# One refinement step moved from the inverse to the right sides, in a DeltaNet and expert layer kernel

## The chip, the cores and the metric

One core of a Trainium2 chip runs the whole layer. The metric is the device time of one execution in microseconds.

## What is computed

The input is 2 sequences of 2048 tokens of 256 channels, cut into 32 chunks of 128 tokens. The layer is a gated delta-rule attention (16 value heads, 8 key heads, head size 128), followed by a mixture of 16 experts with 8 chosen and a shared one. The part that matters here is the recurrence:

```python
def step(state, inp):
    q_t, k_t, v_t, g_t, b_t = inp
    state = state * jnp.exp(g_t)[..., None, None]
    kv_mem = jnp.einsum('bhk,bhkv->bhv', k_t, state)
    delta = (v_t - kv_mem) * b_t[..., None]
    state = state + k_t[..., None] * delta[:, :, None, :]
    out = jnp.einsum('bhk,bhkv->bhv', q_t, state)
    return (state, out)
```

Within a chunk of 128 tokens the deltas of one head solve a triangular system (I + L) Z = R, where L holds the decayed products of the keys and R the right sides (values less what the carried state already gives). Everything is float32, and results have to agree with the float32 reference.

## The kernel before

The 16 value heads are worked on in 4 groups of 4. An *item* is one group of one chunk. In each item the program runs stages of several items at once, so that the engines overlap: `a` (projection, convolution taps, gates of the item three ahead), `f` (front: norms, key products, decays, the triangle L, two ahead), `i` (the inverse, one ahead), `s` (state: solve, output, new state, the item itself), `p` (output projection, one behind), and per chunk `c` (the next chunk's norm and betas) and `e` (experts of the chunk before). Each engine has its own function `item`, which writes its order out by hand; engines meet through semaphores, and every queue is strictly in order. The loop body holds 6 chunks and runs 5 times; the rest is unrolled before and behind it.

The inverse of I + L is built by doubling. GpSimd computes the inverses of the 16x16 diagonal blocks (`base_inverse`), which go through DRAM (`triangle_out`, `blocks_in`, `inverses_out`, `inverses_in`, issued by the sync engine), because the blocks have to change partitions. Three levels follow on TensorE. In each, `invert_q` multiplies, VectorE masks (`mask_q`), and `invert_xt` and `invert_x` add to the transposed inverse XiT and the inverse Xi, which ScalarE copies out of PSUM (`inverse_t`, `inverse`). `turned` (L566) multiplies it by the identity to get the inverse itself, `residual` (L573, L575) forms I - (I + L)X in plain float32 and one fp32r product, and `correct` (L582) adds X times this residual. VectorE copies the result to Tt (L1164), in float32.

The state stage takes two heads at a time (p = 0 and 1). `ks_qs` multiplies keys and queries with the state into banks bS and bD, `right_side` forms R (VectorE), `solve` multiplies by Tt in float32 (L604), `solved` copies Z (ScalarE), `az` and `new_state` form the output and the state's increment, `update_o` and `update_s` finish them on VectorE. `query_state` scales the queries' part on ScalarE. PSUM's eight banks are shared, so most steps also wait until the bank's last content has been read; expert steps, transposes and projections take turns on bB in the order B_ORDER.

## Time and profile before

| | |
|---|---|
| median of 3 runs | 3428.59 us (3428.09 to 3431.92) |
| the profiled execution's own time | 3419.12 us |
| its span, first to last instruction | 3417.3 us |
| mean granted TensorE clock | 0.984 |
| TensorE, VectorE, ScalarE, GpSimd busy | 94%, 80%, 71%, 63% |

An engine's busy time counts the time in which at least one of its instructions runs. TensorE's are pipelined: the next one starts long before the record of the last one ends, so its cost is the distance between starts. Lines such as L604 are lines of the kernel; an operation is named by what it writes and reads (bS<-R,Tt).

### The profile page before, as it was taken

To read this page: it belongs to the slowest core of one execution; us is meant where nothing else is said; L and a number is where in the kernel's file an instruction comes from. 1 tells how busy PE (TensorE), PEld (TensorE's weight loads), DVE (VectorE), ACT (ScalarE), POOL (GpSimd) and SP (SyncE) were. 2 spreads that over 40 slices of the span, in tenths; PEclk is the share of its full clock that TensorE was granted. 3 is DMA by queue.
4 is the path that set the end of the run, shared out by engine and by line. 5 is a ranking of instruction groups with operands and counts; after the bars stand their busy time and mean duration, and the time that the engine had idled before them with its cause. 6 is when DMAs were issued, how large, how long until landed. Compare 5 with 4: busy or idle time off the path is not lost.

```text
span 3417.3 us, 85191 instructions
## 1 busy us (share of the span) xinstructions
PE 3227.1 (94%) x23968; PEld 2867.9 (84%) x24096; DVE 2733.4 (80%) x8720; ACT 2417.5 (71%) x5922; POOL 2149.9 (63%) x5380
## 2 busy tenths in 40 slices
PE   4999999999999999999999999999999999999985
PEld 3888888888888888888888888888888888888874
DVE  4788888888888888788888878888888888888873
ACT  3777777776777777777777767777777777777762
POOL 2766666666666667566666666666666666666650
PEclk8999999999999999999999999999999999999996
DMA  4111111111111111111111111111111111111110
GB/s 179 37 44 37 44 39 34 44 41 39 40 44 34 44 41 37 37 47 35 38 47 37 37 45 38 38 46 39 37 46 35 39 44 41 36 44 38 38 42 4
DMA packets 424217, 145.70 MB, mean 43 GB/s; under 512 B 211168, under 2 KB 421664, under 8 KB 423200
## 3 DMA queue, kind: packets, MB, share of 16 engines
q1 hardware_dynamic: 423712, 139.83, 15.7%
q8 instruction: 211, 3.46, 0.4%
q14 instruction: 294, 2.41, 0.2%
HBM read 93.11 MB, written 46.66 MB: 41 GB/s over the span
## 4 chain that ended last, share of the span: by engine, by line
PE 66%; ACT 13%; issue 7%; DVE 6%; POOL 4%; DMA 3%; SPq 0%; POOLq 0%; ACTq 0%; DVEq 0%
PE bF L466 8%; PE bB L637 6%; PE bQ L547 5%; ACT L811 4%; PE bXT L555 4%; PE bB L693 3%; PE bS L604 3%; PE bB L687 3%; PE bF L477 3%; PE bF L479 3%; PE bD L619 3%; PE bS L612 3%; PE bS L596 2%; PE bX L560 2%; PE bD L597 2%
## 5 line engine op out<-in xcount | busy, mean ns | idle before, releaser
L1105 DVE SCALAR_TENSOR_TENSOR Y<-bF,Cv,Y 128x127 f32<-128x127 f32 (+2 forms) x3072 | 851.6, 339 | 8.2 <-ACT Y L828 3.1
L466 PE MATMUL bF<-XnT,Wqkv 128*128 128x128 f32 x4096 | 534.5, 278 | 0.5 <-ACT XnT L947 0.5
L466 PEld LDWEIGHTS bF<-XnT,Wqkv 128*128 128x128 f32 x4096 | 508.2, 194 | 9.7 <-issue 2.1
L828 ACT ACTIVATE Y<-bF,Cv 128x128 f32<-128x128 f32 x1024 | 385.8, 457 | 103.7 <-PE bF L466 100.3
L898 ACT ACTIVATE XiT<-bXT 128x512 fp32r<-128x512 f32 x384 | 229.0, 596 | 304.5 <-PE bXT L555 300.3
L1533 POOL TENSOR_TENSOR Tp<-Tp 32x64 f32<-32x64 f32 (+2 forms) x768 | 361.4, 471 | 60.2
L1148 DVE TENSOR_TENSOR Qi<-bQ,Cf 128x512 fp32r<-128x512 f32 x384 | 264.0, 688 | 97.7 <-PE bQ L547 96.3
L811 ACT ACT_TABLE_LOAD x257 | 329.7, 1283 | 5.3 <-PEq L1617 0.7
L555 PE MATMUL bXT<-Qi,Xi 128*128 128x128 f32 x1536 | 302.4, 319 | 2.4 <-DVE Qi L1148 2.4
L555 PEld LDWEIGHTS bXT<-Qi,Xi 128*128 128x128 f32 x1536 | 222.4, 192 | 96.4 <-DVE Qi L1148 47.3
L1526 POOL TENSOR_TENSOR Tp<-Yb,Tm 32x64 f32<-32x64 f32 (+1 forms) x384 | 275.4, 717 | 30.1
L1526 POOL TENSOR_TENSOR Tp<-Cb,Yb 32x64 f32<-32x64 f32 (+1 forms) x384 | 274.7, 715 | 30.5 <-POOL Yb L1535 0.8
L1541 POOL TENSOR_TENSOR Yb<-Cb,Cf 32x8 fp32r<-32x8 f32 x128 | 25.9, 202 | 414.4 <-DMA Cb<-DL 414.4
L547 PE MATMUL bQ<-XiT,LnR 128*128 128x128 f32 x1536 | 240.8, 279 | 19.5 <-ACT XiT L898 19.5
L547 PEld LDWEIGHTS bQ<-XiT,LnR 128*128 128x128 f32 x1536 | 211.9, 191 | 47.8 <-ACT XiT L898 28.8
L1427 POOL TENSOR_TENSOR Ln<-Ex,KKQ 128x512 f32<-128x512 f32 x128 | 164.1, 1282 | 129.6 <-issue 111.7
L637 PE MATMUL bB<-Wout,CoT 128*128 128x256 f32 x1024 | 244.2, 382 | 0.9 <-ACT CoT L934 0.8
L905 ACT ACTIVATE Xi<-bX 128x512 fp32r<-128x512 f32 x384 | 226.7, 590 | 2.8 <-PE bX L566 2.3
L1460 POOL TENSOR_TENSOR HG<-LnbG,Lnk 128x4 f32<-128x4 f32 x128 | 25.9, 203 | 299.1 <-ACT Lnk L861 299.1
L637 PEld LDWEIGHTS bB<-Wout,CoT 128*128 128x128 f32 x1024 | 185.9, 192 | 21.6 <-ACT CoT L934 1.1
L974 ACT ACTIVATE Rl<-bB 128x512 f32<-128x512 f32 x128 | 76.5, 597 | 158.4 <-PE bF L688 158.4
L604 PE MATMUL bS<-R,Tt 128*128 128x128 f32 x1024 | 166.8, 286 | 8.3 <-DVE Tt L1164 8.1
(198 smaller groups left out, 9338.8 us busy)
## 6 DMA issues: line engine op xcount, KB each, us to landing
DL<-Ln SPq DMA_DIRECT2D x128, 256.0 KB, 2.2
XiT<-DX SPq DMA_DIRECT2D x128, 256.0 KB, 2.7
Xi<-DX SPq DMA_DIRECT2D x128, 256.0 KB, 3.2
DX<-Yb SPq DMA_DIRECT2D x256, 32.0 KB, 1.9
Xf<-x SPq DMA_DIRECT2D x32, 128.0 KB, 2.8
Wqkv<-wqkv SPq DMA_DIRECT2D x4, 1024.0 KB, 18.0
Cb<-DL SPq DMA_DIRECT2D x128, 32.0 KB, 1.9
Xr<-x SPq DMA_DIRECT2D x32, 128.0 KB, 3.0
```

Of the source, the lines that this page charges most:

```text
L466: last = mm(bank[:, i, :], Wqkv[:, k, c:c + P], XnT[:, k, :], start=(k == 0), stop=(k == KT - 1))
L547: last = mm(heads(bQ)[:, h, :], LnR[:, h, :], XiT[:, h, :], start=True, stop=True)
L555: last = mm(heads(bXT)[:, h, :], Xi[:, h, :], Qi[:, h, :], start=False, stop=True, skip_group_check=True)
L604: last = mm(heads(bS)[:, i, :], Tt[:, 2 * p + i, :], R[:, i, :], start=True, stop=True)
L637: last = mm(bB[:, 0:HID], CoT[:, h, :], Wout[:, g * GH + h, :], start=(h == 0), stop=(h == GH - 1))
L811: nc.scalar.add_instruction(mybir.InstLoadActFuncSet(name=nc.get_next_instruction_name(), act_func_set_id=TABLES[name], engine=mybir.Engin ...
L828: last = op(Y[:, tile, :], bank[:, i, :], ACT.Identity, scale=c[:, TAPS - 1:TAPS], bias=c[:, TAPS:TAPS + 1])
L898: op(XiT[:, :, :], heads(bXT), ACT.Copy).then_inc(sem["xt_done"], 1)
L1105: last = stt(y, bank[:, i, 0:P - shift], Cv[:, g * TILES + tile, n:n + 1], y, ALU.mult, ALU.add)
L1148: tt(Qi[:, :, :], heads(bQ), level, ALU.mult).then_inc(sem["q_done"], 1)
L1526: then(tt(view(Tp[:, :], p * m ** 3, [[m * m, m], [m, m], [1, m]]), pair(left, p), pair(right, p), ALU.mult))
L1533: then(tt(lo, lo, hi, ALU.add))
```

## The change

The inverse is no longer refined. The third level adds to the inverse Xi instead of to its transpose, and ScalarE rounds it to Tt in fp32r (`inverted`). The refinement is made on the right sides: R is rounded to Rr (`rounded_r`), a first solve in fp32r gives Z (`first_z`), VectorE subtracts it from R (`left`), `check` multiplies -L by Z in plain float32, VectorE adds it (`residual`, rounded to Rr), and a second fp32r solve adds to the same bank (`correct`). The solve, the output and the state are done for four heads at once. The orders of TensorE, ScalarE and VectorE are written anew, and the experts' steps are spread differently over the items. Some buffers share memory (Hn with Xn, LaT with Rg), with the waits that this needs.

```diff
@@ sync: inverses_in
-                sp.wait_ge(sem["c_full"], at("c_full", ahead(f, -1)))
+                sp.wait_ge(sem["x_full"], at("x_full", ahead(f, -1)))
@@ tensor
             def invert_x(v, n):
+                if n == LEVELS - 1:
+                    pe.wait_ge(sem["q_done"], at("q_done", v))
+                    pe.wait_ge(sem["xi_done"], at("xi_done", v))
                 for h in range(GH):
                     last = mm(heads(bX)[:, h, :], Qi[:, h, :], Xi[:, h, :], start=False, stop=True, skip_group_check=True)
                 last.then_inc(sem["x_full"], 1)
-            def turned(v):
...
-            def residual(v):
...
-            def correct(v):
...
-            def solve(w, p):
...
+            def solve(w):
+                pe.wait_ge(sem["tt_done"], at("tt_done", w))
+                pe.wait_ge(sem["rr_done"], at("rr_done", w))
                 for h in range(GH):
+                    last = mm(heads(bS)[:, h, :], Tt[:, h, :], Rr[:, h, :], start=(h == 0), stop=True, skip_group_check=True)
+                last.then_inc(sem["zs_full"], 1)
+
+            def check(w):
+                pe.wait_ge(sem["z1_done"], at("z1_done", w))
+                pe.wait_ge(sem["qg_done"], at("qg_done", w))
+                pe.wait_ge(sem["neg_done"], at("neg_done", w))
                 for h in range(GH):
+                    last = mm(heads(bD)[:, h, :], Ln[:, w[1] % 2, h, :], Z[:, h, :], start=True, stop=True)
+                last.then_inc(sem["lz_full"], 1)
+
+            def correct(w):
+                pe.wait_ge(sem["rf_done"], at("rf_done", w))
                 for h in range(GH):
+                    last = mm(heads(bS)[:, h, :], Tt[:, h, :], Rr[:, h, :], start=False, stop=True, skip_group_check=True)
+                last.then_inc(sem["zf_full"], 1)
@@ scalar
+            def inverted(v):
+                act.wait_ge(sem["x_full"], at("x_full", v))
+                act.wait_ge(sem["zf_full"], at("zf_full", ahead(v, -1)))
+                op(Tt[:, :, :], heads(bX), ACT.Copy).then_inc(sem["tt_done"], 1)
+            def rounded_r(w):
+                act.wait_ge(sem["r_done"], at("r_done", w))
+                op(Rr[:, :, :], R[:, :, :], ACT.Copy).then_inc(sem["rr_done"], 1)
+
+            def first_z(w):
+                act.wait_ge(sem["zs_full"], at("zs_full", w))
+                op(Z[:, :, :], heads(bS), ACT.Copy).then_inc(sem["z1_done"], 1)
@@ vector
-            def refined(v):
...
+            def left(w):
+                dve.wait_ge(sem["z1_done"], at("z1_done", w))
+                tt(R[:, :, :], R[:, :, :], Z[:, :, :], ALU.subtract).then_inc(sem["left_done"], 1)
+
+            def residual(w):
+                dve.wait_ge(sem["lz_full"], at("lz_full", w))
+                dve.wait_ge(sem["left_done"], at("left_done", w))
+                tt(Rr[:, :, :], R[:, :, :], heads(bD), ALU.add).then_inc(sem["rf_done"], 1)
```

The new orders, with the stages' letters and the group in which a step of the chunk or the experts stands:

| engine | order in an item |
|---|---|
| TensorE | ks_qs; D2 (3); proj 0,0 and 0,1; ss; kkq; ktr; proj 1,0; **solve**; core_t; parts_t; vtr; exponents; **check**; hT (1); proj 1,1; invert_begin; q0; **correct**; gc (1); xt0; G1 (2), G3 (3); x0; ffn1 (1); q1; out_proj; xt1; D3 (3); x1; az; G0 (1); xnT (0); q2; D1 (2); new_state; laT (3); G2 (2); z_proj; D0 (1); ffo (3); x2; ba (0) |
| ScalarE | query_state; key_norm; **rounded_r**; last_tap 0; keys; ba (1); **first_z**; parts_t; core_t; scales; values; decays; hT (1); last_tap 1; XiT 0; ffn1 (1), G3 (3), G1 (2); Xi 0; norm (0); **solved**; XiT 1; norm1 (0); Xi 1; rounded_l; G0 (1), laT (3); square_o; G2 (2); xnT (0); activated; norm2 (0); ffo (3); out_norm; **inverted** |
| VectorE | ended; D0 (2); x1, ba, hn (1); right_side; squares; D2 (3); gated; products; taps; sp (1); **left; residual**; taps; mask 0; gc (1); taps; norm (0); shared (1); mask 1; scores (1); taps; U3 (3); accumulate; U1 (2); xn (0); D3, la (3); D1 (2); update_o; route (1), norm1 (0); update_s; U0 (1); mask 2; gate_bias; out_norm; ffo, result (3); U2 (2) |
| GpSimd | as before, but the scaled keys come behind the negated triangle |

Before, x1 and ba of VectorE stood at the end of group 0's item, D2 in group 2's, and `z_proj` had the third transposed product, xnT, `turned` and `residual` around and behind it.

## Rows read from the trace of the kernel before

**Rows 1.** The page's first part: busy us (share of the span) xinstructions of each engine.
```profile
PE 3227.1 (94%) x23968; PEld 2867.9 (84%) x24096; DVE 2733.4 (80%) x8720; ACT 2417.5 (71%) x5922; POOL 2149.9 (63%) x5380
```

**Rows 2.** Windows, one chunk and its four items: length, then each engine's busy us, PEclk.
```profile
1703.32:1805.47 102.15, 99.57 (x750) 88.74 (x753) 85.87 (x274) 75.42 (x186) 68.90 (x172) 1.00 0.16 40
1703.32:1727.86 24.54, 24.49 (x186) 21.91 (x186) 21.18 (x61) 17.89 (x43) 17.07 (x44) 1.00 0.15 37
1727.86:1751.61 23.75, 22.34 (x158) 19.44 (x158) 20.59 (x72) 17.42 (x47) 15.15 (x40) 1.00 0.19 50
1751.61:1779.19 27.58, 26.77 (x207) 24.17 (x206) 23.48 (x82) 20.09 (x53) 20.27 (x48) 1.00 0.15 39
1779.19:1805.47 26.28, 25.97 (x205) 23.22 (x206) 20.62 (x62) 20.02 (x46) 16.41 (x42) 1.00 0.14 35
```

**Rows 3.** TensorE in order of time, group 0: start us, us, instructions, idle before.
```profile
1728.72 1.95 PE L466 MATMUL bF<-XnT,Wqkv 128*128 128x128 f32 x16
1730.80 1.05 PE L494 MATMUL bXT<-Cf,Sq 128*128 128x1 f32 x8
...
1733.68 0.71 PE L604 MATMUL bS<-R,Tt 128*128 128x128 f32 x4 [0.19 <-DVE Tt L1164]
1734.23 1.06 PE L466 MATMUL bF<-XnT,Wqkv 128*128 128x128 f32 x8
...
1740.30 0.66 PE L555 MATMUL bXT<-Qi,Xi 128*128 128x128 f32 x4
1740.80 0.61 PE L560 MATMUL bX<-Xi,Qi 128*128 128x128 f32 x4
1741.65 0.66 PE L547 MATMUL bQ<-XiT,LnR 128*128 128x128 f32 x4 [0.24 <-ACT XiT L898]
...
1748.11 1.02 PE L479 MATMUL bF<-Wz,XnT 128*128 128x512 f32 x2
1749.93 0.66 PE L566 MATMUL bX<-IdR,XiT 128*128 128x128 f32 x4 [0.80 <-ACT XiT L898]
1750.43 1.10 PE L573 MATMUL bQ<-XiT,Ln 128*128 128x128 f32 x8
1751.29 0.48 PE L575 MATMUL bQ<-XiT,NegR 128*128 128x512 f32 x1
1751.61 0.60 PE L596 MATMUL bS<-S,QK 128*128 128x256 f32 x2
```

**Rows 4.** Groups of VectorE, shapes apart: shapes xcount | busy us, mean ns | idle before.
```profile
L1180 DVE TENSOR_TENSOR O<-Qg,bS 128x256 f32<-128x256 f32 x256 | 105.6, 412 | 7.8 <-PE bS L612 7.8
L1164 DVE COPY Tt<-bX 128x512 f32<-128x512 f32 x128 | 88.2, 689 | 1.2 <-PE bX L582 0.9
...
L1299 DVE TENSOR_TENSOR Rl<-bF,Rl 128x512 f32<-128x512 f32 x128 | 87.2, 681 | 22.5 <-ACT Rl L976 22.4
```

**Rows 5.** The same view for ScalarE.
```profile
L898 ACT ACTIVATE XiT<-bXT 128x512 fp32r<-128x512 f32 x384 | 229.0, 596 | 304.5 <-PE bXT L555 300.3
...
L917 ACT ACTIVATE Z<-bS 128x256 f32<-128x256 f32 x256 | 102.3, 400 | 18.8 <-PE bS L604 18.8
...
L894 ACT ACTIVATE LnR<-Ln 128x512 fp32r<-128x512 f32 x128 | 79.3, 620 | 0.0
```

**Rows 6.** ScalarE in order of time, the same item of group 0.
```profile
1730.12 0.63 ACT L844 ACTIVATE Sq<-QK 128x512 f32<-128x512 f32 x1
...
1734.76 0.65 ACT L912 ACTIVATE Qg<-bD,Sc 128x128 f32<-128x128 f32 x2
...
1735.52 0.33 ACT L876 ACTIVATE PartsT<-bXT 128x128 bf16<-128x128 bf16 x1
...
1737.07 0.68 ACT L889 ACTIVATE Ex<-bQ 128x512 f32<-128x512 f32 x1
```

**Rows 7.** TensorE's waits (us, times, longest), and its order in time one item later.
```profile
PE bXT L537 <- DMA Xi<-DX: 11.3, 10, 2.2
...
1762.90 0.48 PE L537 MATMUL bXT<-XiT,IdR 128*128 128x512 f32 x1
```

444 lines of the change are left out of this document (198 added, 246 removed).

## The prediction, made before the changed kernel was run

> **What bounds the kernel now.** I read the page's busy shares first. TensorE works 94% of the span, VectorE 80%, ScalarE 71%, GpSimd 63% [rows 1]. An average hides stages, so next I cut one chunk of 128 tokens out of the steady loop and split it at the start of each item (an item is one group of four heads). The chunk takes 102.15 us, TensorE is busy 99.57 of them, VectorE 85.87, ScalarE 75.42. The four items take 24.54 (group 3), 23.75 (group 0), 27.58 (group 1) and 26.28 us (group 2), because the expert stage is spread unevenly over them, and the granted clock is 1.00 throughout [rows 2]. TensorE bounds three of them plainly. In group 1 VectorE has 23.48 us of work in 27.58, the fullest it gets.
>
> Then I read TensorE's own order of time in the group 0 item [rows 3]. What counts there is the distance from start to start. A record lasts 0.27 us, but 16 instructions of 128 columns pass in about 1.79 us (L466: 1.95 less the tail of the last, 0.27 - 0.11) and 8 in 0.86 (L573, 1750.43 to 1751.29), so each takes 0.11 us whether it is one pass of a plain float32 product (two instructions for each product) or a whole fp32r product (one). Four fp32r products therefore take 0.50 (L555, 1740.30 to 1740.80), one of 512 columns 0.32 (L575). Gaps of less than 0.17 us hide inside the records. Read from the starts, the group 0 item waits about 0.3 before L494 (1728.72 plus 1.79 is 1730.51, it starts at 1730.80), 0.35 before L604, 0.4 before L547 at 1741.65 and 0.9 before L566 (L479 takes 0.91), with two small ones some 2.3 us in all. Reading the three other items in the same way I get 1.7, 1.4 and 0.7. So a chunk is about 96 us of TensorE work and 6 us of waits.
>
> **The parts on TensorE.** For each item the change takes out: the third transposed inverse (four fp32r products, 0.50), the turning product L566 (0.50), the residual L573 and L575 (0.86 + 0.32), the correction of the inverse L582 (four fp32r, as L566, 0.50) and the two-pass solve L604 (twice four instructions, 0.55 each by the one shown, 0.44 by count) [rows 3]. That is 28 instructions of 128 columns and one of 512. It adds a third product for the inverse itself, a first solve and a correcting solve (four fp32r each, 0.50) and a residual on the right sides (eight instructions, 0.86): 20 instructions. By count the difference is 8 x 0.11 + 0.32 = 1.2 us, by the starts 3.78 - 2.36 = 1.4 us, since blocks of both kinds alternate less often. I take 1.3 us for each of 128 items: 166 us, or 5.2 a chunk. ks, qs, az and the new state keep their counts; four heads at once only joins them.
>
> The 0.11 us is worth a second look. The Trainium skill, "TensorE: Matmul & The Clock Gate", section "Back-to-back issue gap", gives about 81 ns for each matmul of 128 columns in a stream of weight loads and matmuls. The starts in [rows 3] show 0.11 us, so the trace disagrees; by the page's figure the eight instructions would be worth 0.65 us instead of 0.88.
>
> **The parts elsewhere.** VectorE loses a 512-wide copy (L1164), the fourth mask and two 256-wide output updates (L1180), and gains a subtraction, the residual's addition and one 512-wide update, each taken as L1299 [rows 4]. Out go 0.69 + 0.69 (the mask taken as the copy) + 0.82, in come 3 x 0.68: -0.2 us an item, which I cost at nothing, as it is hidden behind TensorE. ScalarE loses one inverse copy (0.60, L898 [rows 5]) and gains the rounding of the right side (0.62, as L894) and two 512-wide Z at 0.60 where two 256-wide stood at 0.40 (L917), +0.4: +0.4 us an item, 1.7 a chunk on 75.42. GpSimd's scaled keys become one instruction of the same size, and are moved behind the negated triangle: nothing, as the new state wants them only some 17 us into the item. The sync queue's load of the inverses now waits for a product that is issued some 4 us earlier, which can only help. VectorE: x1, with its statistics and ba, moves from the end of group 0's queue to the head of group 1's, in front of the right side. That puts an estimated 2.4 us more of VectorE work into group 1 (five to eight operations of 0.2 to 0.45 us each), and queued behind it stands the right side, for which rounding and solve wait.
>
> **The waits that are added.** The solve is now a chain within the item: ks, right side (DVE), rounding (ACT), solve, first Z (ACT), residual (PE, DVE), correcting solve, Z (ACT), az. On its own it needs about 11 us and has 24; what matters is where each in-order queue has got to. With T the start of an item on TensorE I walk group 0. ScalarE: Sq ends at 2.9 as now (1730.12 + 0.63, T being 1727.86) [rows 6]; then out_norm and the last copy of the inverse (3.9), four query-state scalings at 0.25 a start (two take 0.50 from 1734.76) to 4.9, key_norm 5.5, rounding 6.1, last_tap 1.4 to 7.5, keys 7.9, first Z 8.5, PartsT 8.8. Today PartsT is there at 8.0 (1735.52 + 0.33). TensorE: ks and qs 1.7, projection 3.5, ss 4.3, kkq and ktr 5.4, projection 6.3, solve 6.8, core_t 7.2; then parts_t wants the keys (7.9), exponents wants PartsT (8.8), and the residual follows at 9.3, when its Z has been there since 8.5. Without waits it would have started at 8.2. So some 1.1 us are lost before the residual against 0.6 today in the same place. Behind it VectorE wants the product at about 9.5 and gets it at 10.2, then has taps (1.3) and mask 0 ready at 12.3, just when TensorE asks for it (12.2). Mask 1 comes behind eight taps, at 15.3 to 16.5, where TensorE, with out_proj done, wants it at 16.2. That item comes to about 23.2 us. The same walk gives 26.7 for group 1 (VectorE is the later one: D0 waits for the gated product that stands behind route and the state update), 24.1 for group 2 and 25.3 for group 3, which takes over D2. Sum 99.4 against 102.15: -2.8 us a chunk. This walk is probably slow by a few tenths an item, since it lets most operations take their record's length where starts are closer. The other end is that no wait is added: -5.2. I take -3.6, nearer the walk, because its waits lie at named places: 5.2 of work saved, 1.6 us of new waits.
>
> **Sum.** A chunk's worth for each of 32 chunks: -3.6 x 32 = -115 us. The profiled execution took 3419.1 us (span 3417.3), so 3304; the median of the runs before, 3428.6, lies 9.5 above it, so 3314.
>
> **The rivals.** (a) *All of it and more.* The wait of 0.9 us before L566 goes away with the turning product (and it is the longest one seen in [rows 3]); if no new one comes, the chunk gains 5.2 + 0.9: 3428.6 - 195 = 3234, or 3260 with a part of it. For it: the saving is plain instruction count on the engine that bounds. Against: ScalarE gains work ahead of the keys, 0.6 for the rounding and 0.6 for the inverse's copy at least. (b) *VectorE takes over in group 1.* Its 23.48 us [rows 2] plus the 2.4 moved in are 25.9, and it always has some waits at its residual and at shared; if that makes the item 27.5 and the others stay near 24.5, the chunk is 100.8 and the time 3428.6 - 1.35 x 32 = 3385. (c) *Slower: the hand-overs of the solve.* TensorE's queue is in order; if rounding, first Z and residual arrive late by an operation of their engine (0.62, 0.60, 0.68), all that stands behind the solve, the residual or the correction waits. With two of three late the new waits are 0.4 + 1.3 us an item against 1.3 saved: +0.4 x 128 = 51 us, 3480. It decides once the added waits pass 1.3 us an item. Against it: the projection, ss, kkq, core_t and vtr stand between these steps. (d) *The inverse's way through DRAM.* Ex ends at 9.9 after T today (1737.07 + 0.68 [rows 6]) and the next item's L537 starts at 1762.90, 25.2 us later; TensorE waited for this transfer only ten times, 11.3 us in all [rows 7]. In the walk Ex ends about 1 us later and items are 0.9 shorter, while the block is wanted 0.5 later: about 1.4 us of slack goes, and the trace doesn't show that more than that was there. If it binds, the gain is eaten to about zero: 3428. (e) *It isn't single-pass:* L555 passes four heads' products in four instructions already [rows 3], so I give this nothing.
>
> **How the numbers follow.** Forecast 3314 (3284 to 3345) 0.54; (a) 0.20; (b) 0.12; (d) 0.04; (c) 0.10. A difference below 0.2%, 7 us, is about what a measurement of this kernel can't tell from none. Faster 0.86, same 0.04, slower 0.10. The range takes in (a) and (b), 3240 to 3390, and leaves out (c) and (d).
>
> **What would show it.** In the trace after: TensorE's work down, with a third of L555, L566, L573, L575 gone and the solve's group half as long for each product; items of about 23, 26.7, 24 and 25.3 us; waits before parts_t, exponents and the residual of about 1 us; VectorE over 95% busy in group 1. I am wrong if TensorE is idle for over 2 us an item at the solve or the correction, or if L537 waits for its DMA in most items.

## The result, and the profile after

The changed kernel takes 3522.12 us (median of 4 runs, 3519.54 to 3526.05) against 3428.34 us (4 runs, 3428.06 to 3431.92): ratio 1.0272, 95% interval 1.0254 to 1.029. It is slower by 94 us where 115 us less was forecast; the time lies above the range, and above rival (c)'s 3480. The profiled execution took 3519.54 us with a span of 3517.7.

The page's busy line of the changed kernel, its chain of work that ended last, by engine, and below that the same chain in the kernel before:

```profile
PE 3183.2 (90%) x22944; PEld 2758.5 (78%) x22944; DVE 2813.6 (80%) x8591; ACT 2465.3 (70%) x5922; POOL 2139.8 (61%) x5252
...
PE 32%; DVE 28%; ACT 26%; issue 12%; DMA 1%; POOL 1%; DVEq 1%; ACTq 0%; SPq 0%; POOLq 0%
```

```profile
PE 66%; ACT 13%; issue 7%; DVE 6%; POOL 4%; DMA 3%; SPq 0%; POOLq 0%; ACTq 0%; DVEq 0%
```

Against [rows 1], TensorE is 44 us less busy in a span that is 100 us longer, and VectorE 80 us busier although it has fewer instructions. TensorE now holds a third of the chain, where it held two thirds.

The windows view of one chunk of the changed kernel and of its items in groups 1, 2, 3 and 0 (columns as in [rows 2]: window, its length, busy time of PE, PEld, DVE, ACT, POOL, granted clock, DMA share, GB/s):

```profile
1699.93:1805.26 105.33, 97.38 (x720) 84.54 (x719) 88.10 (x269) 76.94 (x186) 66.79 (x165) 1.00 0.16 39
1699.93:1728.84 28.91, 26.20 (x195) 22.73 (x195) 26.29 (x84) 21.42 (x54) 19.13 (x44) 1.00 0.15 37
1728.84:1753.79 24.95, 23.94 (x190) 21.17 (x189) 18.30 (x57) 18.48 (x43) 15.39 (x40) 1.00 0.15 37
1753.79:1780.68 26.89, 25.05 (x187) 21.90 (x186) 22.59 (x61) 19.91 (x46) 17.06 (x42) 1.00 0.14 34
1780.68:1805.26 24.58, 22.19 (x156) 18.74 (x155) 20.93 (x70) 17.14 (x46) 15.21 (x41) 1.00 0.19 48
```

The chunk is 3.2 us longer than in [rows 2]: group 0 +0.8, group 1 +1.3, group 2 -1.3, group 3 +2.4. TensorE's longest waits in the changed kernel (waited for: us in total, times, longest):

```profile
PE bXT L555 <- DVE Qi L1139: 68.5, 117, 2.6
PE bXT L507 <- ACT Kn L850: 33.9, 65, 0.6
PE bXT L494 <- ACT Sq L827: 26.6, 34, 2.9
...
PE bB L680 <- DVE Y L1121: 24.3, 55, 0.5
PE bB L686 <- DVE Rl L1289: 23.1, 53, 2.2
PE bB L630 <- DVE As L1259: 22.8, 31, 0.7
PE bB L686 <- DVE Acc L1201: 21.4, 31, 0.7
...
PE bS L584 <- ACT Rr L902: 3.7, 3, 1.8
...
PE bXT L537 <- DMA Xi<-DX: 2.9, 2, 1.7
```

Two of them in the kernel before:

```profile
PE bXT L494 <- ACT Sq L844: 18.6, 49, 2.3
PE bXT L555 <- DVE Qi L1148: 2.4, 4, 0.8
```

The new solve's own steps hardly wait (L584 3 times; the residual L592 and the correction L598 0.2 and 0.8 us in all), and the way of the inverse through DRAM still less than in [rows 7]. What grew most is L555, TensorE's wait for mask 0: 2.4 us in the whole kernel before, 68.5 now.

How much work went? TensorE's weight loads, one for each product instruction, fell from 24096 [rows 1] to 22944, which is nine an item: the eight of 128 columns (0.11 us each) and the one of 512 (0.32) that the prediction counted. That is 1.2 us an item and 4.8 us a chunk, an estimate from the distances between starts. As the chunk is 3.2 us longer all the same, some 8.0 us of waits came. Reading the long gaps off the starts gives less, some 5.3 us of waits a chunk before and 11.7 now, since a short gap can't be told from work.

The timeline around mask 0 in group 2 of the changed kernel (GpSimd, VectorE and TensorE, other lines left out):

```profile
1738.96 1.28 POOL L1412 TENSOR_TENSOR Ln<-Ex,KKQ 128x512 f32<-128x512 f32 x1 [2.17 <-ACT Ex L872]
...
1739.92 0.56 PE L547 MATMUL bQ<-XiT,LnR 128*128 128x128 f32 x4
1740.20 1.04 POOL L1474 TENSOR_TENSOR Kd<-Kn,Sc 128x512 f32<-128x512 f32 x1
...
1740.32 0.61 PE L598 MATMUL bS<-Rr,Tt 128*128 128x128 f32 x4
1740.58 0.22 DVE L1111 SCALAR_TENSOR_TENSOR Tails<-bF,Cf,Bk 128x12 f32<-128x12 f32 x1
1740.71 0.68 DVE L1139 TENSOR_TENSOR Qi<-bQ,Cf 128x512 fp32r<-128x512 f32 x1
1741.20 1.27 POOL L1412 TENSOR_TENSOR AT<-Ex,KKQ 128x512 f32<-128x512 f32 x1
1741.31 1.19 DVE L1121 TENSOR_TENSOR Y<-Y,Hd 128x12 f32<-128x12 f32 x1
...
1741.44 0.66 PE L555 MATMUL bXT<-Qi,Xi 128*128 128x128 f32 x4 [0.52 <-DVE Qi L1139]
```

Two things are to be seen. Between the first square L547 and L555 there is only the correction, 0.4 us, and the mask takes longer than that. And first_tokens (L1121), an addition over 12 columns, takes 1.19 us and ends when GpSimd's AT ends, 1742.47. In the kernel before the same addition, at 1741.42, took 0.16 us, in group 0's item; AT had ended at 1740.38. The group of this addition in the kernel before, and in the changed one (busy us, mean ns | idle before):

```profile
L1129 DVE TENSOR_TENSOR Y<-Y,Hd 128x12 f32<-128x12 f32 x256 | 79.9, 312 | 0.0
```

```profile
L1121 DVE TENSOR_TENSOR Y<-Y,Hd 128x12 f32<-128x12 f32 x256 | 161.5, 631 | 0.4 <-issue 0.4
```

That is VectorE's growth: 82 us. The change put the scaled keys Kd, 1.04 us, between Ln and AT on GpSimd, and moved AT so far back that it now meets this addition: 114 of the 256 additions begin while AT runs, and every one of these ends 0.02 to 0.03 us behind it.

### The profile page after: what moved, and what is told of

It reads as the page before. It is cut to its first block, busy times and chain, and to the rows that moved or that the text cites. A ratio compares the mean times of both kernels' runs of the same rounds, so it can differ in the third digit from the quotient of the medians.

```text
span 3517.7 us, 81544 instructions
## 1 busy us (share of the span) xinstructions
PE 3183.2 (90%) x22944; PEld 2758.5 (78%) x22944; DVE 2813.6 (80%) x8591; ACT 2465.3 (70%) x5922; POOL 2139.8 (61%) x5252
## 4 chain that ended last, share of the span: by engine, by line
PE 32%; DVE 28%; ACT 26%; issue 12%; DMA 1%; POOL 1%; DVEq 1%; ACTq 0%; SPq 0%; POOLq 0%
DVE Y L1097 13%; ACT L794 5%; ACT Y L811 5%; PE bB L630 5%; PE bB L680 4%; PE bS L606 3%; PE bB L686 3%; DVE Y L1121 3%; PE bX L563 2%; DVE Qi L1139 2%; ACT Rr L902 2%; DVE R L1159 2%; PE bF L466 2%; PE bQ L547 2%; ACT Qg L897 2%
## 5 line engine op out<-in xcount | busy, mean ns | idle before, releaser
L1097 DVE SCALAR_TENSOR_TENSOR Y<-bF,Cv,Y 128x127 f32<-128x127 f32 (+2 forms) x3072 | 853.9, 339 | 81.8 <-ACT Y L811 72.6
L466 PE MATMUL bF<-XnT,Wqkv 128*128 128x128 f32 x4096 | 523.7, 276 | 0.0
L466 PEld LDWEIGHTS bF<-XnT,Wqkv 128*128 128x128 f32 x4096 | 498.5, 193 | 7.0 <-issue 1.9
L881 ACT ACTIVATE XiT<-bXT 128x512 fp32r<-128x512 f32 x256 | 152.9, 597 | 288.1 <-PE bXT L555 288.1
L1412 POOL TENSOR_TENSOR Ln<-Ex,KKQ 128x512 f32<-128x512 f32 x128 | 164.8, 1287 | 287.8 <-ACT Ex L872 287.8
L630 PE MATMUL bB<-Wout,CoT 128*128 128x256 f32 x1024 | 276.3, 417 | 24.3 <-DVE As L1259 22.8
L563 PE MATMUL bX<-Xi,Qi 128*128 128x128 f32 x1536 | 259.4, 292 | 4.1 <-DVE Qi L1139 0.7
L563 PEld LDWEIGHTS bX<-Xi,Qi 128*128 128x128 f32 x1536 | 209.8, 194 | 57.5 <-DVE Qi L1139 33.2
L547 PE MATMUL bQ<-XiT,LnR 128*128 128x128 f32 x1536 | 238.0, 278 | 8.4 <-ACT XiT L881 8.4
L555 PE MATMUL bXT<-Qi,Xi 128*128 128x128 f32 x1024 | 183.0, 302 | 68.5 <-DVE Qi L1139 68.5
L630 PEld LDWEIGHTS bB<-Wout,CoT 128*128 128x128 f32 x1024 | 201.6, 207 | 54.3 <-issue 27.2
L547 PEld LDWEIGHTS bQ<-XiT,LnR 128*128 128x128 f32 x1536 | 214.0, 193 | 28.1 <-ACT XiT L881 13.4
L555 PEld LDWEIGHTS bXT<-Qi,Xi 128*128 128x128 f32 x1024 | 146.6, 195 | 98.3 <-DVE Qi L1139 90.5
L686 PEld LDWEIGHTS bB<-Rw,Rl 128*128 128x128 f32 x1024 | 127.4, 195 | 86.9 <-issue 60.7
```

Source lines behind the costliest of these rows:

```text
L466: last = mm(bank[:, i, :], Wqkv[:, k, c:c + P], XnT[:, k, :], start=(k == 0), stop=(k == KT - 1))
L547: last = mm(heads(bQ)[:, h, :], LnR[:, h, :], XiT[:, h, :], start=True, stop=True)
L555: last = mm(heads(bXT)[:, h, :], Xi[:, h, :], Qi[:, h, :], start=False, stop=True, skip_group_check=True)
L563: last = mm(heads(bX)[:, h, :], Qi[:, h, :], Xi[:, h, :], start=False, stop=True, skip_group_check=True)
L630: last = mm(bB[:, 0:HID], CoT[:, h, :], Wout[:, g * GH + h, :], start=(h == 0), stop=(h == GH - 1))
L686: last = mm(bB[:, i * LAT:(i + 1) * LAT], Rl[:, i, :], Rw2[:, n * EG + i, :], start=True, stop=True)
```

## The experiments

All times are medians; ratios are against the kernel before, run in the same job. To compare the kernels inside the loop I took the starts of L494 in every item from the trace and added up the four groups' medians over items in which the granted clock was 1.00 throughout ("undisturbed"); beside it stands the mean chunk, and the number of stretches at half the clock (1.2 instead of 2.4 GHz) between the items 8 and 120. Where these stretches are many, few undisturbed items are left (28 of each group is all): in e9 one in one group and four in another, in e13 four in one, in e6 six in one. The kernel before's own median moved between 3424.07 and 3428.34 from job to job, so differences below 10 us are read from the ratios.

| kernel | us | ratio (95%) | undisturbed | mean chunk | half-clock |
|---|---|---|---|---|---|
| before | 3428.34 | 1 | 102.17 | 102.74 | 3 |
| after | 3522.12 | 1.0272 (1.0254-1.029) | 105.22 | 106.03 | 13 |
| e1 keys first | 3478.90 | 1.0145 (1.0127-1.0163) | 103.09 | 104.55 | 19 |
| e2 late tokens | 3516.09 | 1.0251 (1.0225-1.0278) | 104.06 | 105.97 | 21 |
| e3 before, early tokens | 3480.64 | 1.0156 (1.0135-1.0176) | 104.08 | 104.76 | 4 |
| e6 no refinement | 3499.36 | 1.021 (1.0179-1.0242) | 101.49 | 105.17 | 39 |
| e9 before, no refinement | 3444.80 | 1.0049 (1.0032-1.0066) | 99.79 | 103.91 | 49 |
| e13 = e9 + filler | 3421.03 | 0.9988 (0.9977-0.9998) | 100.49 | 103.03 | 29 |
| e15 = e6 + filler | 3447.79 | 1.0081 (1.0057-1.0106) | 102.35 | 103.48 | 6 |
| e12 = e1 + filler | 3474.87 | 1.0155 (1.0136-1.0174) | 103.56 | 104.35 | 7 |
| e5 = e1, cover for mask 0 | 3532.15 | 1.0305 (1.0279-1.0331) | 105.43 | 106.26 | 11 |
| e8 = e1, az up | 3479.38 | 1.0156 (1.013-1.0181) | 103.23 | 104.67 | 15 |
| e10 = e5 and e8 | 3533.43 | 1.0309 (1.0284-1.0333) | 104.88 | 106.26 | 16 |
| e17 = e1, x1 back | 3469.93 | 1.0139 (1.012-1.0158) | 102.97 | 104.28 | 14 |
| e18 = e1, projection up | 3534.84 | 1.032 (1.0299-1.0341) | 104.04 | 106.22 | 25 |
| e19 = e1, rounding late | 3532.10 | 1.0303 (1.0284-1.0322) | 104.63 | 106.15 | 27 |
| e20 = e19, O early | 3528.70 | 1.0295 (1.0278-1.0312) | 104.58 | 106.07 | 24 |
| e21 = e18 and e20 | 3566.99 | 1.0417 (1.0397-1.0438) | 105.03 | 107.25 | 28 |
| e22 = e1, ScalarE's block | 3584.43 | 1.0471 (1.0448-1.0493) | 104.60 | 107.73 | 32 |
| e24 = e22, e17, filler | 3551.26 | 1.0367 (1.035-1.0384) | 104.89 | 106.95 | 23 |

### GpSimd's order

e1 undoes one move of the change, the scaled keys behind the negated triangle:

```diff
                     before_first(a)
+                if state:
+                    decay_keys(w)
                 if front:
                     minus_l(f)
-                if state:
-                    decay_keys(w)
-                if front:
                     attention(f)
```

> The changed kernel with one edit: GpSimd's scaled keys stand in front of the negated triangle again, as in the kernel before, so the output decays AT run about 1.0 us earlier. In the trace of the changed kernel VectorE's first_tokens (Y<-Y,Hd, L1121) takes 631 ns in the mean instead of 312, up to 1.2 us where it starts together with GpSimd's AT, and ends with it. Theory A (VectorE is held by GpSimd's long operation, and this is on the path): AT now ends at about the start of first_tokens, the mean falls to 350 ns or less, and up to 80 us come back: 3440 to 3465. Theory B (the loss is the new hand-overs of the solve and the new order of TensorE, the held operation is hidden): the mean may fall, the time stays at 3505 to 3525.

Measured: 3478.90, that is 43 us less. The undisturbed items are 2.1 us a chunk shorter, 68 us in 32 chunks; stretches at half the clock, 19 instead of 13, go with the difference. The addition is short again, and TensorE's wait for it (L680) is gone, but L555 still waits for mask 0:

```profile
L1121 DVE TENSOR_TENSOR Y<-Y,Hd 128x12 f32<-128x12 f32 x256 | 49.7, 194 | 0.4 <-issue 0.4
```

```profile
PE bXT L555 <- DVE Qi L1139: 51.8, 99, 1.3
PE bXT L507 <- ACT Kn L850: 30.3, 59, 0.6
```

e2 leaves GpSimd alone and moves the addition behind the next four taps instead:

```diff
-                if new:
-                    first_tokens(a, 0)
...
                     taps(a, 1, 2)
+                    first_tokens(a, 0)
                     taps(a, 1, 1)
```

> The changed kernel with another edit for the same cause: GpSimd is left alone, and VectorE issues first_tokens of the first half one block of taps (1.1 us) later, behind AT. Theory A: the mean of L1121 falls as in the edit of GpSimd's order, and about as much time comes back, less what the experts' product G waits longer for it in two groups (0.1 to 0.3 us each): 3445 to 3475. Theory B: no change, or slower by G's longer wait, 3515 to 3540.

Measured: 3516.09. The addition takes 211 ns on average, so the collision is gone here too, but the time hardly moves. The experts' product L680 and its pair L681, which overwrites the bank that the taps read, start on a count that this addition raises last. L680 still waits for it (27.4 us, 60 times; 24.3 in the changed kernel, none in e1), now because the addition is issued late. And the undisturbed items did become 1.2 us a chunk shorter, while the mean chunk stayed: the stretches at half the clock went from 13 to 21. So this run says nothing against the collision; the addition's new place in the queue costs about as much.

e3 makes the collision in the kernel before: first_tokens moves up, right behind the tails, onto AT.

```diff
                     tails_out(a, 0)
+                    first_tokens(a, 0)
...
                 if new:
-                    first_tokens(a, 0)
                     taps(a, 1, 2)
```

> The kernel before with one edit the other way: first_tokens of the first half stands right behind tails_out, 1.8 us earlier, where GpSimd runs AT (1739.11 to 1740.38 in the trace of before, first_tokens would start at 1739.6). Theory A: its mean rises from 312 to about 600 ns or more, mask 0 and the second right side behind it come 0.5 to 0.8 us late in three groups, and the kernel loses 20 to 60 us: 3450 to 3490. Theory B: the mean stays, time 3425 to 3435.

Measured: 3480.64, 52 us more, by one addition of 0.16 us moved. Its lines and TensorE's wait in e3:

```profile
L1129 DVE TENSOR_TENSOR Y<-Y,Hd 128x12 f32<-128x12 f32 x256 | 174.3, 681 | 0.0
```

```profile
PE bXT L555 <- DVE Qi L1148: 57.1, 98, 0.9
```

Unheld, an addition of 0.16 us moved up in each of 128 items could cost 20 us at most (an estimate), so over 30 of the 52 are the hold. In e1 nothing but GpSimd's order was changed. So the collision is a cause by itself, in either order, and worth 43 us in the changed kernel. The Trainium skill, "SBUF — State Buffer", section "SBUF: two separate sides", says that VectorE and GpSimd share a pair of ports with an exclusive lock for the whole instruction, and that a VectorE operation with two inputs in SBUF contends for it with a GpSimd operation that reads SBUF, as AT does. The addition has both inputs in SBUF, the mask (one input in PSUM) at 1740.71 ran 0.68 us beside Kd: the traces agree.

### Is it the work on TensorE?

e6 leaves the refinement out of the changed kernel: the residual's product, both operations of VectorE, the correcting solve and the second Z. The solution is only as exact as its first solve.

```diff
-                if state:
-                    check(w)
...
-                if state:
-                    correct(w)
...
-                if state:
-                    solved(w)
...
-                if state:
-                    left(w)
-                    residual(w)
```

> The changed kernel without its refinement (the product check, left, residual, the correcting solve and the second copy of Z are left out; the result is the first solve's, so less exact). It takes 12 instructions and 1.3 us of TensorE, 1.3 us of VectorE and 0.6 us of ScalarE out of each item. If TensorE's work sets the time, as the prediction had it, -165 us: about 3355. Theory B (the time is set by hand-overs of the refinement): more than that, 3300 or below. Theory A (the VectorE queue with its held operation sets it): between, as VectorE's two operations go too but the held one may stay: 3360 to 3420.

Measured: 3499.36. That is 1.3 us of TensorE work out of each of 128 items, 170 us, and 23 us gained. Its undisturbed items are 3.7 us a chunk shorter, of 5.3 taken off TensorE. Not all of that is TensorE's, since VectorE loses two operations as well and the addition is held less (327 ns on average instead of 631). But 39 stretches at half the clock take most of it back: the mean chunk is only 0.9 us shorter. e9 does the same to the kernel before: the third transposed inverse, its turning, the residual, the correction and the fourth mask are left out, and the plain last product stands in their place, some 2.2 us an item.

```diff
-                if state:
-                    correct(w)
...
                 if invert:
-                    invert_xt(v, 2)
+                    invert_x(v, 2)
...
-                if invert:
-                    turned(v)
-                    residual(v)
```

> The kernel before with its refinement of the inverse left out (the third transposed inverse, its turning, the residual, the correction and the fourth mask; the plain product for the last level stands in their place, so the solution is only as exact as the unrefined inverse). That takes some 2.2 us of TensorE work out of each item of the old order. Theory A, TensorE's work bounds the old order as the profile of before suggests: about 2.0 us an item, 128 items, 3140 to 3190. Theory B, the other engines' hand-overs stand right behind the work there too, as they did in the new order where leaving 1.3 us an item out gained only 23 us in all: 3300 to 3400.

Measured: 3444.80, slower than the kernel before by 0.49%. This is the plainest verdict of the study: 280 us of work taken off the engine that was 94% busy, and nothing gained. Its items without half clock add up to 99.79 instead of 102.17, so 2.4 of 8.8 us a chunk come through as time and 6.4 turn into waits (a rough split, as few undisturbed items are left in two groups). The first of its waits stands at L494, which waited 18.6 us before:

```profile
PE bXT L494 <- ACT Sq L842: 138.7, 124, 4.3
PE bB L696 <- DVE Rl L1293: 39.8, 28, 2.2
```

And the rest is lost again: the mean chunk is 4.1 us above the undisturbed items.

### The clock

Two stretches of e6 from one L494 to the next, both beginning in an item of group 2, one in which the granted clock falls and one in which it doesn't, and below them six microseconds at the same place of each (here the disturbed one first):

```profile
1508.02:1533.40 25.38, 23.93 (x185) 20.74 (x184) 17.74 (x55) 19.42 (x45) 16.62 (x41) 1.00 0.13 34
1713.52:1741.94 28.42, 27.21 (x185) 23.44 (x184) 17.49 (x55) 19.17 (x44) 16.63 (x41) 0.88 0.14 36
```

```profile
1723.00:1729.00 6.00, 6.00 (x31) 5.24 (x29) 3.32 (x12) 2.06 (x4) 3.04 (x12) 0.50 0.10 16
1517.50:1523.50 6.00, 6.00 (x56) 5.68 (x52) 4.37 (x15) 3.31 (x7) 3.03 (x12) 1.00 0.10 16
```

TensorE issues 31 instructions instead of 56 (its output projection L631 takes 3.61 us instead of 1.94), and the way from L494 to L494 is 3.0 us longer. Ahead of the fall TensorE had waited 0.28 us at L537 and 0.79 at L555. In the other it had waited as long (0.28 and 0.78), so these waits alone don't decide it. To test it, work is added: products of constants that nobody reads, where TensorE waits.

```diff
+            def fill(ps, lo, n):
+                for i in range(n):
+                    mm(heads(ps)[:, lo + i % (GH - lo), :], IdR[:, 0, :], IdR[:, 0, :], start=True, stop=True)
...
                 if front:
+                    pe.wait_ge(sem["xt_done"], at("xt_done", ahead(f, -2)))
+                    fill(bXT, 0, 9)
                     ss(f)
```

> The kernel before without its refinement, as in e9_before_no_refinement, and in each item nine products of constants (128 columns each, about 1.0 us together, their result is read by nobody) ahead of the sums of squares L494, where TensorE waited for ScalarE's squares 124 times, 138.7 us in all. Nothing else is changed: work is added. Theory C, the clock: without the refinement TensorE waits more, and its granted clock falls to half in about half of the items, which gives back what the shorter items saved; filled waits keep the clock at 1.00. Then the chunk falls from 103.9 us to about 100, the time to 3320 to 3360. Theory D, only the hand-overs count and the low clock is harmless: the filler lies in a wait, so it changes nothing or costs up to what it overhangs, 3445 to 3500.

Measured: 3421.03, 24 us less than e9, with 128 us more of TensorE work in it. The half-clock stretches fall from 49 to 29, and most of those left are in the items of group 1, where the gap ahead of L494 was 2.5 us from start to start in e9 and is still 1.6. The undisturbed items got 0.7 us a chunk longer, the mean chunk 0.9 shorter.

e15 adds four products ahead of the transposed parts and nine behind the first square to e6, e12 the same four, and five behind the correcting solve (`fill(bD, 0, 5)`), to e1:

```diff
                 if front:
+                    pe.wait_ge(sem["tt_done"], at("tt_done", ahead(f, -2)))
+                    fill(bX, 0, 4)
                     parts_t(f)
...
                     invert_q(v, 0)
+                if state:
+                    pe.wait_ge(sem["qg_done"], at("qg_done", w))
+                    fill(bD, 0, 9)
```

> The changed kernel without its refinement, as in e6_no_refinement, and with products of constants that nobody reads in its two regular waits: four (0.44 us) ahead of the transposed parts and nine (1.0 us) between the first square and the product L555 that waits for mask 0. Theory C, the clock: the half-clock stretches that stand in 40 places of the loop go, the chunk falls from 105.3 us to about 101.7, the time to 3380 to 3400. Theory D: the low clock is harmless, 3500 to 3560.

> The changed kernel with the scaled keys ahead of the negated triangle (e1_kd_first), refinement kept, and products of constants that nobody reads in two waits: four (0.44 us) ahead of the transposed parts, five (0.55 us) behind the correcting solve, ahead of the wait for mask 0 (51.8 us over 99 items). Theory C, the clock: the 19 half-clock stretches of the loop go and with them 1.4 us a chunk: 3430 to 3450. Theory D: the filler overhangs the waits here and there: 3480 to 3520.

Measured: e15 3447.79, 52 us less than e6, stretches from 39 to 6; e12 3474.87, no different from e1 (ratios 1.0155 and 1.0145), stretches from 19 to 7, with undisturbed items 0.5 us a chunk longer since the filler overhangs its waits. Theory C holds in its sign in e13 and e15, but neither reaches its number, and in e12 it fails. In e12 what the clock gives back the filler takes.

### What else bounds the item

The next runs move work without adding or leaving out any. e5 puts the second projection between the first square and L555; e8 puts az ahead of the output projection and ScalarE's last Z up with it; e10 does both.

```diff
-                if new:
-                    proj(a, 1, 1)
                 if invert:
                     invert_begin(v, front)
                     invert_q(v, 0)
+                if new:
+                    proj(a, 1, 1)
```

```diff
                     invert_q(v, 1)
+                if state:
+                    az(w)
                 if post:
                     out_proj(u)
```

> This is the kernel with the scaled keys ahead of the negated triangle on GpSimd, and one more move: TensorE's second projection (proj(a, 1, 1)) goes from in front of the first square q0 to behind it, so that it lies between q0 and xt0, where the changed kernel has only the correcting solve (0.44 us). Theory A, the hand-overs: in the new order xt0 is asked for too soon behind q0, and TensorE waits for mask 0 at L555 in 99 items, 51.8 us in all; with the projection in between the wait goes in three of four groups, the time falls by 45 to 65 us, to 3415 to 3435. Theory B, the work: TensorE is bound elsewhere and the wait only moves on to the next product that VectorE or ScalarE must hand over; then the time stays at 3465 to 3485. If last_tap 1 on ScalarE, which now comes about 1 us later, is wanted by what stands behind it, it gets slower, 3490 or more.

> The same kernel with the scaled keys first, and the product az moved from behind the inverse's own product to right behind the second square q1, ahead of the output projection; ScalarE's last copy of Z goes up with it, right behind last_tap 1. It gives cover ahead of the output projection, which in group 1 waits for the shared gating (L630, 22.7 us over some 30 items), and behind q1, where mask 1 is waited for. Theory A, the hand-overs: these waits go down by 25 to 40 us, 3440 to 3455. Theory B: the cover that az gave where it stood is missed there, and the waits only change places: 3470 to 3490.

> Both moves in one kernel: the second projection between q0 and xt0, az and the last Z ahead of the output projection, the scaled keys ahead of the negated triangle. Theory A, the hand-overs: the gains add up, 3375 to 3405, faster than the kernel before, since the change's own saving of some 0.85 us of TensorE work in each item then shows. Theory B, the work has moved to another engine or the order as such is no better: 3450 or more.

Measured: e5 3532.15, 53 us more than e1. The wait for mask 0 fell from 99 times to 34, as meant, and came back behind it, at L686 (39.2 us for the accumulation, 21.4 before it) and at L537. e8 3479.38, as e1: cut at the start of L573, its group 1 is 0.8 us shorter, and groups 2, 3 and 0 are 0.5, 0.3 and 0.2 us longer. e10 3533.43, as e5, though the wait for mask 0 is all but gone in it (3.8 us, 5 times); L547 waits 47.7 us instead. The covers are not what is missing.

e17 moves the expert stage's x1 and the projection's ba on VectorE back to the end of group 0:

```diff
-                if e and g == 1:
-                    experts(t - 1, "x1", 0)
-                if c and g == 1:
-                    chunk_front(t + 1, "ba")
...
+                if e and g == 0:
+                    experts(t - 1, "x1", 0)
+                if c and g == 0:
+                    chunk_front(t + 1, "ba")
```

> The changed kernel with the scaled keys first (e1_kd_first), and on VectorE the expert stage's x1 (a normalization, a residual and statistics) and the projection's ba moved back from the head of group 1's queue to the end of group 0's, where the kernel before has them. Theory A: group 1's item, 28.7 us in the new order against 27.6 in the old, is long because VectorE's right side and the solve's whole chain stand behind them; it falls to about 27.5, and the time to 3440 to 3455. Theory B: they wait for ScalarE's norm and TensorE's product anyway and only lengthen group 0's item by as much: 3470 to 3490.

Measured: 3469.93, which by the ratios (1.0139 and 1.0145, with intervals that overlap) is no gain that can be told from none. A group 1 item of e17, by the windows view, still takes 28.70 us with 24.06 of VectorE's work in it:

```profile
1882.74:1911.44 28.70, 25.78 (x195) 22.67 (x195) 24.06 (x84) 21.49 (x54) 20.36 (x46) 1.00 0.15 37
```

Then I took a round of engines for the cause (projection, last tap, taps, silu and squares, sums of squares, keys, parts, exponents, next projection). e18 moves the second projection up, ahead of the transposed parts; e19 moves ScalarE's rounding L877, which waits 110 us in all for the third square, behind the activation block; e20 adds VectorE's output update ahead of the experts' D1 in group 2; e21 is all three.

```diff
                 if new:
+                    proj(a, 1, 1)
                 if front:
                     parts_t(f)
```

```diff
                 if invert:
                     inverse(v, 1)
-                if front:
-                    rounded_l(f)
...
                     activated(a)
+                if front:
+                    rounded_l(f)
```

```diff
+                if state:
+                    update_o(w)
                 if e and g == 2:
                     experts(t - 1, "D", 1)
-                if state:
-                    update_o(w)
```

> The changed kernel with the scaled keys first (e1_kd_first), and TensorE's second half projection (proj(a, 1, 1)) moved up, from behind the residual's product to in front of the transposed parts. e5_cover_mask0 moved the same block 1 us down and lost 53 us. Theory E, a round of engines bounds the item (projection, last tap on ScalarE, taps on VectorE, silu and squares on ScalarE, sums of squares on TensorE, keys and parts, exponents, and behind these the next projection, since all queues are in order): the block up shortens the round, ScalarE's 104 us of waits for it (128 times) go, and the wait of 0.5 us for the keys ahead of the parts is covered: 3430 to 3455. Theory B: only TensorE's own work and waits count, and it gains the covered waits alone: 3465 to 3475.

> The same base, and on ScalarE the rounded copy of the negated triangle (LnR, L877) moved from the middle of the item, where it waits 1.15 us in 96 items for TensorE's third square, to behind the activation block. The activation block and the squares stand behind it in ScalarE's queue. Theory E, the round of engines: it shortens the round by 0.5 us or so in three of four groups, 3430 to 3460. Theory B: ScalarE isn't on the path there, or the 0.5 us that the copy now takes ahead of the query states costs the same: 3470 to 3490.

> As e19_late_rounding, and on VectorE in group 2 the output's update (L1170) ahead of the experts' block D1, which it waits behind (1.3 us of ScalarE's wait for it, 31 times, 42 us in all). Theory E: group 2's item falls by 1 us or so more, 25 to 35 us less than e19_late_rounding. Theory B: as e19_late_rounding.

> All three moves together: projection up, rounding late, output's update early. Theory E: the gains add, 3370 to 3420, at or below the kernel before. Theory B: 3465 or more.

Measured: 3534.84, 3532.10, 3528.70 and 3566.99, where e1 stands at 3478.90. The theory fell. In e18 the last tap does start earlier (ScalarE's wait of 104.5 us for the projection is gone), but the projection puts 0.9 us ahead of parts and exponents; L537 then waits for ScalarE's Ex 92 times (27.1 us) and L555 130 times (81.8 us). In e19 the copy now stands in front of the query states: TensorE waits for the keys 98 times instead of 59 (45.6 us instead of 30.3), and 29.0 us instead of 4.2 for VectorE's sums at L501. These 40 us go with most of the 53 lost.

That pointed at ScalarE's unbroken block from the activation to Ex. e22 changes its inner order:

```diff
+                if front:
+                    keys(f)
                 if new:
                     last_tap(a, 0)
-                if front:
-                    keys(f)
...
-                if state:
-                    first_z(w)
                 if front:
                     parts_t(f)
-                if post:
-                    core_t(u)
+                if state:
+                    first_z(w)
                 if front:
                     scales(f)
                     values(f)
                     decays(f)
+                if post:
+                    core_t(u)
```

e24 adds e17's move to it, and four products of constants behind the correcting solve:

```diff
                 if state:
                     correct(w)
+                    fill(bD, 0, 4)
```

> The changed kernel with the scaled keys first (e1_kd_first), and another order inside ScalarE's block between the sums of squares and the exponents, which runs without a pause in the trace (from the table load to Ex some 12 us): the keys ahead of the last tap, the transposed parts ahead of the first Z, the copy of the transposed core behind Ex. No work is added or removed. Theory F: this block bounds the item, since 0.6 us put into it by e19_late_rounding in front of the query states cost 53 us; the keys come 1.4 us, PartsT and Ex 0.5 us earlier, TensorE's waits at the transposed parts go, and the item falls by 0.3 to 0.5 us: 3415 to 3445. Theory G: every queue of this order is tight and the last tap, first Z and core copy that are moved back cost what the others gain: 3470 to 3520.

> e22_scalar_block and e17_x1_back together, with four products of constants that nobody reads (0.44 us) behind the correcting solve, where TensorE waits for mask 0. Theory F with the clock's theory C: the gains add, and the half-clock stretches that follow the wait at L555 go: 3395 to 3430, about the kernel before. Theory G: 3460 to 3520.

Measured: e22 3584.43, the slowest of all, and e24 3551.26. The timeline of e22 shows why one can't go by one engine (VectorE's subtraction of Z and GpSimd's Ln start together), and under it stand Ln's group and TensorE's longest wait:

```profile
1710.37 0.68 DVE L1159 TENSOR_TENSOR R<-R,Z 128x512 f32<-128x512 f32 x1
1710.39 1.81 POOL L1412 TENSOR_TENSOR Ln<-Ex,KKQ 128x512 f32<-128x512 f32 x1 [0.68 <-ACT Ex L872]
```

```profile
L1412 POOL TENSOR_TENSOR Ln<-Ex,KKQ 128x512 f32<-128x512 f32 x128 | 219.4, 1714 | 118.6 <-ACT Ex L872 118.6
```

```profile
PE bXT L555 <- DVE Qi L1139: 105.1, 100, 1.6
```

Ex came earlier, as meant (10.4 us after the item's start instead of 10.6, medians), and so Ln met the subtraction in 125 of 128 items: it took 1714 ns on average instead of 1287 and ended 0.3 us later than in e1, which gives the gain back and more. This is the same collision with the roles changed, GpSimd held by VectorE. The last tap came later and with it the eight taps that stand ahead of the residual and mask 0 on VectorE (it waits 115.9 us for the last tap instead of 67.9), and L555 waits twice as long.

## Why the prediction was wrong

*What bounds the kernel.* This step failed, and the rest with it. A TensorE that is busy 99.57 of 102.15 us [rows 2] was read as the bound, so that work taken from it would come back as time. e9 shows that it doesn't: of some 8.8 us of work a chunk taken away, 2.4 came through in the undisturbed items, and nothing in the time. The records overlap and hide gaps, as the text itself said, and the other engines stood right behind: work at ScalarE, VectorE and GpSimd hands over at fixed places of an in-order queue, and most such places have less slack than the saving.

*The parts on TensorE.* This term was right. The added products took what was forecast: in the group 0 item that begins at 1780.68 the first solve is 0.48 from start to start, the residual 0.89, the correction under 0.5. By count 4.8 us a chunk went, where 5.2 were forecast.

*The parts elsewhere.* "GpSimd's scaled keys ... moved behind the negated triangle: nothing" was wrong, and is the largest single term: 43 us (e1). I asked when the keys are wanted, and not what is moved back behind them (AT, by 1.04 us) and what runs on VectorE then. The rule cited above from the Trainium skill's page spoke against this move, and the prediction didn't weigh it. VectorE's terms were right, since its growth is this addition alone; so was ScalarE's, 0.4 us an item forecast and 47.8 us in all measured.

*The waits that are added.* 1.6 us a chunk were forecast; some 8.0 came by count, 6.4 of them as gaps that can be read off the starts. Up to the residual the walk was good: in the item that begins at 1780.68 its product starts at 9.7 us where the walk had 9.3, and L507, at the parts, waits 33.9 us in all, about 1 us a chunk. It went wrong behind it, at mask 0. TensorE and VectorE there:

```profile
1790.35 1.05 PE L592 MATMUL bD<-Z,Ln 128*128 128x128 f32 x8
1791.62 0.69 DVE L1164 TENSOR_TENSOR Rr<-R,bD 128x512 fp32r<-128x512 f32 x1
1792.22 1.11 DVE L1097 SCALAR_TENSOR_TENSOR Y<-bF,Cv,Y 128x125 f32<-128x125 f32 x4
1793.00 0.61 PE L598 MATMUL bS<-Rr,Tt 128*128 128x128 f32 x4
1793.38 0.68 DVE L1139 TENSOR_TENSOR Qi<-bQ,Cf 128x512 fp32r<-128x512 f32 x1
1794.12 0.66 PE L555 MATMUL bXT<-Qi,Xi 128*128 128x128 f32 x4 [0.51 <-DVE Qi L1139]
```

The walk had mask 0 ready at 12.3, when TensorE asks for it at 12.2, and so no wait. It is ready at 13.4 (1793.38 + 0.68), and TensorE, which begins the correction at 12.3, is through with it at about 12.8. Of the 1.1 us, 0.7 is a slip in the walk's own figures: from the product at 10.2 the taps (1.3) and the mask (0.68) alone make 12.2, and the residual's addition L1164, 0.69 us, which stands between, is left out. The rest is that the product came 0.4 late. At mask 1 the walk had 15.3 to 16.5, wanted at 16.2; it ran from 17.4 to 18.1, wanted at 17.0, because the held addition (1.20 us) and the statistics of the next chunk's norm (0.8 us) stand ahead of it besides the eight taps.

The items were forecast at 23.2, 26.7, 24.1 and 25.3 (groups 0 to 3); with the collision out (e1) they are 23.6, 28.7, 24.4 and 26.4, medians measured at the same cut as [rows 2]. Groups 0 and 2 were walked well, groups 1 and 3 are 2.0 and 1.1 off. In these the experts' steps lie between; the prediction gives their sums only, so the steps can't be compared.

*The clock.* "The granted clock is 1.00 throughout" [rows 2] was read as a given. In the kernel before, stretches at half the clock are rare (3); in the changed kernel there are 13, in e1 19, in e6 39, in e9 49. No term of the sum had it.

*The sum of what happened.* From before to after the mean chunk grew by 3.3 us, 105 us in 32 chunks; the spans differ by 100. Of these, 43 us are the collision (e1). What is left in e1, 1.8 us a chunk, is half undisturbed items (103.09 against 102.17) and half what the mean lies above them (1.5 against 0.6). The second half goes with 19 stretches instead of 3; that all of it is the clock is not shown.

*The rivals.* (a) is out. (b) VectorE taking over in group 1 named the item that came out longest (28.9 us, where it had 27.5) but was wrong in its cause: e17 took the 2.4 us out again and the item stayed. VectorE was busy 91% there, not 95. (c) had the sign, at 0.10, and its condition (waits over what is saved) was met, at places other than the solve. (d) is out by the L537 row; (e) is out. That the range left out (c) and (d), all that was slow, rested on the first step. Smaller slips changed nothing: the four items add up to 99.3 and not 99.4, (b)'s to 101.0 and not 100.8, and (a)'s 3234 lies outside the range that is said to take it in.

*Still open.* Why four undisturbed items of the new order take 0.9 us more than four of the old, with less work on TensorE; the wait for mask 0, 51.8 us in e1, is the largest that is left, but covering it (e5) only moved it. Six moves of single blocks (e5, e8, e17, e18, e19, e22) gained nothing that stands clear of the noise and cost up to 105 us; no single place bounds it that I found. Why the clock falls in one item and not in its like is open too. None of the kernels run beats the kernel before by over 0.2%; e13 comes to 0.9988 of it, without its refinement.

## What to carry to other kernels

A busy share of 97% doesn't say that an engine's work is the bound: leave a piece of that work out once, before costing an edit by instruction counts. When an operation moves on GpSimd or VectorE, look at what its neighbours then overlap with on the other of the two, in both directions. When you walk the queues, write down every operation of each queue; one left out can be as large as the whole slack. And on TensorE a saving can be eaten by the clock, so ask where the freed time will stand as a wait.

## What the runs showed of the hardware

- A VectorE addition with both inputs in SBUF that starts while GpSimd's AT runs ends with it: 0.16 us alone, 1.19 beside AT, and so in all 114 cases in the changed kernel. The other way round, GpSimd's Ln took 1.81 us instead of 1.28 when VectorE's subtraction, also with both inputs in SBUF, started 0.02 us ahead of it (e22). The masks, VectorE operations with one input in PSUM, took 0.67 to 0.69 us in all 384 cases, whatever GpSimd did.
- Adding useless products to each item made two kernels faster: 1.0 us an item gave 24 us (e9 to e13), 1.4 us an item gave 52 us (e6 to e15), as stretches at half the clock went from 49 to 29 and from 39 to 6. In a third kernel (e1 to e12, 1.0 us) they went from 19 to 7 and the time stayed.
- At half the clock six microseconds held 31 matmuls instead of 56, and the way from one L494 to the next took 28.42 us instead of 25.38.
